# Turning a pair's outputs at the end of the odd block's list, in an AdaLN attention and expert kernel

## The reference

```
logits = h @ gate_w.T; each token goes to its 2 best of 8 experts
per (batch, expert), at most 256 tokens:
  q = (xe @ q_w.T) through two small maps, multiplied;  k likewise, with the expert's k_w;  v = xe @ v_w[e].T
  linear attention over chunks, 8 heads of 16:
    o = (q k^T * causal) v + q S;   S = S + k^T v
out[token] = sum of its two experts' rows, weighted; normalised per head; @ o_w.T
x = x + ga * out
```

## Time and profile before

| what | value |
|---|---|
| median of 3 runs (lowest, highest) | 1153.3 us (1145.38, 1154.67) |
| the profiled execution's own time | 1154.31 us |
| its span, first to last instruction | 1152.6 us |
| mean granted clock of TensorE | 0.969 |
| busy: PE, DVE, ACT, POOL | 1030.0, 903.6, 665.7, 512.3 us |

### The profile page before, as it was taken

The page is one execution under the profiler, slowest core; times in us unless marked ns, Lnnn a source line. Parts: engine busy times, 40 slices in busy tenths (PEclk is TensorE's granted clock), DMA queues, the critical chain, the costliest instruction groups (busy, mean ns, idle before and its releaser), DMA issues.

```text
span 1152.6 us, 23833 instructions
## 1 busy us (share of the span) xinstructions
PE 1030.0 (89%) x7766; PEld 721.8 (63%) x7766; DVE 903.6 (78%) x2107; ACT 665.7 (58%) x1651; POOL 512.3 (44%) x477
## 2 busy tenths in 40 slices
PE   6776888899998789999998989989998999899997
PEld 4554565566665556666665657657776677677774
DVE  5885677899985667887798877898889887877764
ACT  2543455556655566767675755646675665555563
POOL 2074154503334542132212237858886554466551
PEclk9997899999998999999999999989999999999997
DMA  9997133323333332222222233232533052214320
GB/s 301 354 399 106 56 123 108 124 76 102 107 104 101 97 94 74 69 77 74 64 72 63 56 108 111 74 101 70 139 103 101 12 158 83 80 54 115 104 71 18
DMA packets 87047, 124.00 MB, mean 108 GB/s; under 512 B 11280, under 2 KB 70160, under 8 KB 82832
## 3 DMA queue, kind: packets, MB, share of 16 engines
q1 hardware_dynamic: 76688, 97.30, 28.1%
q0 software_dynamic: 10240, 25.18, 7.6%
HBM read 71.32 MB, written 51.13 MB: 106 GB/s over the span
## 4 chain that ended last, share of the span: by engine, by line
PE 50%; DVE 27%; ACT 9%; issue 8%; another core or an unknown queue 5%; DMA 0%; DVEq 0%; POOL 0%; SPq 0%; ACTq 0%; POOLq 0%
PE bank L1433 6%; PE wide L1457 6%; PE bank L1719 5%; PE bank L1517 5%; PE bank L1709 5%; PE wide L1709 5%; DVE epp L1795 4%; PE bank L1501 3%; DVE kvw L1802 3%; DVE att L1559 2%; PE bank L1509 2%; PE bank L1420 2%; PE bank L1447 1%; ACT epp L1770 1%
## 5 line engine op out<-in xcount | busy, mean ns | idle before, releaser
L1672 POOL TENSOR_TENSOR kvw<-kvw,hq 128x512 f32<-128x512 f32 x128 | 171.3, 1338 | 150.7 <-ACT kvw L1762 150.4
L261 POOL DMA_INDIRECT routed_rows<-hq,idxs x128 | 131.2, 1025 | 232.5 <-DVE att L1559 98.7
L921 POOL DMA_INDIRECT gst<-attended_rows,idxs x128 | 135.2, 1057 | 203.4 <-DVE att L1559 100.2
L1559 DVE SCALAR_TENSOR_TENSOR att<-reach,endrel,wide 128x1024 f32<-128x1024 f32 x152 | 194.4, 1279 | 22.3 <-PE wide L1457 12.6
L1795 DVE TENSOR_TENSOR epp<-kvw,epp 128x512 fp32r<-128x512 f32 x160 | 142.9, 893 | 77.7 <-ACT epp L1770 75.6
L1719 PE MATMUL bank<-epp,w2p 128*128 128x512 f32 x480 | 162.7, 448 | 8.3 <-DVE epp L1795 8.1
L1770 ACT ACTIVATE epp<-kvw 128x512 fp32r<-128x512 f32 x160 | 100.8, 630 | 94.6 <-DVE kvw L1802 89.9
L1709 PE MATMUL bank<-hp,w1p 128*128 128x512 f32 x480 | 140.3, 401 | 0.0
L1709 PE MATMUL wide<-hp,w3p 128*128 128x512 f32 x480 | 138.5, 397 | 0.0
L1433 PE MATMUL bank<-kvw,turned 128*128 x304 | 131.1, 513 | 5.7 <-ACT turned L1321 2.7
L1762 ACT ACTIVATE kvw<-bank 128x512 f32<-128x512 f32 x160 | 94.7, 592 | 57.0 <-PE wide L1709 55.9
(11 more groups left out here) (265 smaller groups left out, 1876.6 us busy)
## 6 DMA issues: line engine op xcount, KB each, us to landing
hq<-weight_rows SPq DMA_DIRECT2D x16, 2048.0 KB
rows<-routed_rows SPq DMA_DIRECT2D x76, 256.0 KB
routed_rows<-zero SPq DMA_DIRECT2D x2, 7168.0 KB
attended_rows<-ob SPq DMA_DIRECT2D x76, 128.0 KB
routed_rows<-zero SPq DMA_DIRECT2D x1, 5120.0 KB, 19.2
out<-fin SPq DMA_DIRECT2D x16, 256.0 KB, 2.4
routed_rows<-hq,idxs POOLq DMA_INDIRECT x128
gst<-attended_rows,idxs POOLq DMA_INDIRECT x128
```

The source lines that it names most:

```text
L261: pool.indirect_dma_start(hs[s], bass.IndirectOffsetOnAxis(idxs[:, t, k:k + 1], 0), hq[:, t, :], None, bounds_check=BLOCKS[s] * P - 1, oob ...
L921: pool.indirect_dma_start(gst[:, u, k, :], None, orow[s], bass.IndirectOffsetOnAxis(idxs[:, t, k % TOPA:k % TOPA + 1], 0), bounds_check=BL ...
L1559: dve.scalar_tensor_tensor(out=att[:, n % 2, :, :], in0=reach[:, :, :].rearrange("p a c -> p (a c)").unsqueeze(1) .to_broadcast([P, 4, 2 * ...
L1672: pool.tensor_tensor(g, g, rows_of(1 - b % 2, n, n + 1), ALU.mult).then_inc(s_eu, 1)
```

## The change

`turn_outputs(h)` moves from between `keys_values` and `turn_k` to the very end of TensorE's list of an odd n, behind `carried(n+1)`. `output_rows(h)` moves from behind `split_heads` to the end of ScalarE's list, behind the post copies and the post work. ScalarE's copy of the turned k gets a semaphore of its own, `s_kk`, one count a pair. TensorE's `turn` now waits for that in place of `s_kx`, which comes after the two head copies. `turn_outputs(h)` waits until the copy of pair h + 2's turned k is done (count h + 3), where it waited for the copy `turned` of pair h + 3.

```diff
+        s_kk = sem("turned_k_copied")
...
-                act.activation(k_turned(g), bank[0][:, 0:2 * P].rearrange("p (a c) -> p a c", c=P), ACT.Copy)
+                act.activation(k_turned(g), bank[0][:, 0:2 * P].rearrange("p (a c) -> p a c", c=P),
+                               ACT.Copy).then_inc(s_kk, 1)
...
 # attention_scalar, the loop
-                if odd and here(h):
-                    output_rows(h)
                 exponent(n)
                 linear(n)
                 post_copies(act, n)
                 post_act(act, n)
+                if odd and here(h):
+                    output_rows(h)
...
 # turn(g)
-                    pe.wait_ge(s_kx, g - 1)
+                    pe.wait_ge(s_kk, g - 1)
...
 # turn_outputs(g)
                 pe.wait_ge(s_oc, g + 1)
-                pe.wait_ge(s_te, min(g + 4, PAIRS))
+                pe.wait_ge(s_kk, min(g + 3, PAIRS))
...
 # attention_tensor, the loop
-                if odd and here(h):
-                    turn_outputs(h)
                 if odd and here(h + 2):
                     turn_k(h + 2)
...
                 post_pe(pe, n)
                 if is_block(n + 1):
                     carried(n + 1)
+                if odd and here(h):
+                    turn_outputs(h)
```

## The result

The changed kernel takes 1170.0 us, the median of four runs (1158.19 to 1172.16), against 1152.2 for the one before beside it (1145.38 to 1154.67). The ratio is 1.0147, with a 95% interval of 1.0099 to 1.0195: it is slower, by 11 to 22 us. The forecast was 1161, its range 1144 to 1176: the time lies in the range, 9 us above the forecast.

A forecast was written before the change was run, and what follows sets the result against it. TensorE, busy 89%, was taken as the bound, sharing early attention with VectorE. Terms 11.8, 4.2, 1.2, -1.3 and -9.9 made +6.0 on 1154.3, 1160.3; about 1 for other pairs and the median 1 lower left 1161, range 1144 to 1176.

The forecast's parts named there:

- the hand-off: turn_outputs waits for ScalarE's k copy with scores queued behind: 0.47 late in 25 chain passages before 400 us, +11.8.
- (b): After 400 us, 7 chain passages without post work: oTs is on time, loss 0.6 each, +4.2.
- (c): Turns with the transposes of line 994, 7 passages: scores 0.17 later each, +1.2.
- (d): Turns with the Silu copy, 5 passages: turn_k 0.44 earlier, 0.25 reaching the copy and head splits, -1.3.
- (e): Output product at line 1014 comes 1.3 us earlier, so VectorE's addition at line 1059 stops waiting: -9.9, least sure.
- Rival (1): Slower: the additions' 9.9 us don't come back, plus 3 for output_rows, 1173 us; chance 0.27.
- the late rows: output_rows behind ScalarE's post work, needed by turn in the even list: 0, with +3 as the upper end.
- The rival of a hidden delay: Faster: TensorE waited for VectorE ahead of scores anyway, so idle time at line 1447 is saved; 1139 us, chance 0.12.
- The rule that I cited: Two of TensorE, VectorE, ScalarE cannot use one PSUM bank in the same partition in one cycle; wait can't be dropped.

The follow-up runs named there:

- The outer experiments: On the changed kernel: k copy put first on ScalarE, turn_outputs at the end, 1164.0 us; or turn_outputs waiting for the two head copies too, 1231.9 us.
- TensorE's half: Kernel before with only TensorE's list changed, with the signal and the waits, output_rows left behind split_heads: 1175.4 us, ratio 1.0154.

## Why the prediction was right or wrong

**The sign, the place and, nearly, the size of the hand-off were right.** The sum had +11.8 before 400 us; it is +12.0 at block 76, at 405 us before, of which some 2 to 3 us are the clock, so nearer 9 to 10 for the hand-off. It had 0.47 a pair; the turn at 329 us has 0.50 from the product to `scores`, and the early median is 0.43 more. Where the loop starts was wrong: I had it run from `oTs`'s start to `scores`, 1.24 to become 1.71, and that turn has 2.24 (331.72 - 329.48), as `oTs` comes early there and the chain does not pass it. The chain did not stay at 25 passages there, it now has 33, but they were paid less than in full. `turn_k` follows at 0.65 as forecast, the k copy starts 0.15 behind v's (0.2 assumed), and only the signal is 0.14 to 0.15 where I had 0.05. The outer experiments, removing the wait and lengthening it, both bear out that this step carries most of the loss.

**The late plain turns and the ones of line 994, (b) and (c), were right together**: +4.2 and +1.2. The post work repeats every ten lists. In such a round the intervals between masks say the following (medians over seven rounds, in us; interval 1 is the one behind the mask of block 80, 90 and so on, and has the output product, 3 the Silu copy):

| interval in the round | 1 | 3 | 4 | 5 | 7 | 8 | 9 |
|---|---|---|---|---|---|---|---|
| before | 6.44 | 3.94 | 4.71 | 3.21 | 2.68 | 3.53 | 2.80 |
| after | 6.30 | 3.91 | 4.56 | 3.20 | 3.20 | 3.03 | 3.60 |

Intervals 7 to 9 grow by 0.80 a round on the mean, 5.6 us in seven rounds, against 5.4. Number 9 is the one with line 994 of the earlier trace rows. Its own shift is small, as I had it: in that of block 109 the product stands at 538.91 and `scores` at 541.06, 2.15 apart, against 1.93 before (523.84 to 525.77), 0.22 where the sum had 0.17. The rest of what shows between its masks seems carried over from 7, as 8 looks quick.

**The Silu turns, (d), give less than half** of the -1.3: interval 3 is 0.03 shorter in the median and not shorter on the mean. The chain of the earlier trace rows goes on from the Silu copy over VectorE to the next mask, in interval 4, and that one is 0.16 shorter in the median, 0.5 us over seven rounds.

**The step that failed is (e), the output product, -9.9.** Additions still wait 7.8 us in seven turns (6.4 of it up to 692 us), so 2 us came back. All intervals but 7 to 9 together give back 1.4 us in the seven rounds, where (d) and (e) had 11.2. I had taken an unnamed releaser for TensorE's late product because that was the only signal waited for. The product did come 1.4 us earlier behind the key and value product, and the wait stayed; without the gathers it is gone. The sum without the 7.8 that stayed is 1154.3 + 6.0 + 7.8 = 1168.1, as measured. That agreement is partly luck: the clock added some 2 to 3 us up to block 76, and 2.4 were given back outside the blocks; no step of mine held either. And the range held only because it was wide: the sum had 6 us, the kernel lost 14 in the trace and 18 in the medians.

**Rival (1) named the right reason**, the signal late for another reason than the product, and gave 1173, nearer to 1170 than the forecast. By its own condition, less than 3 us of the additions' waits gone, it is the one that came true. Its 3 us for the late rows can't be seen beside TensorE's half. The rival of a hidden delay falls, since TensorE met VectorE's mask in 6 turns instead of 24.

**A misreading**: the prediction gives line 1447 2% of the chain, 23 us. The earlier trace rows says 1%; its 49 pieces add up to 16.9 us. No term used it.

**Bank 0.** The rule that I cited from the Trainium skill (Advanced Engine Details and Errata, Bank Collisions) could not be tried, as every kernel here waits the sharing out. The other one, from the Trainium skill (Perfetto Trace Analysis, Tensor Engine Instruction), a weight load ahead of matmuls in flight, would have made the loss 5 us smaller. In the turn at 329 us the load of line 1449 starts at 331.35 and its matmul at 331.38, both behind the wait, so the 0.14 was not to be had. Where no wait stands between, loads do start early: in the timeline of the early k copy that of line 1455 starts at 293.22, while the matmuls of `carried` run from 293.11 to 293.49.

**What stays open.** The kernel with the early k copy and `turn_outputs` at the end is slower than the kernel before by 0.5%, and by 4.0 us than the same kernel with `turn_outputs` at its old place. That the transposes at the end stand directly between `carried` and `scores`, with nothing left in the list to make up for them, is my reading; the wait for `oTs` that moved to `carried`, the early k copy itself and the clock are rivals, and no run isolates one. Dropping the wait for the k copy was not tried, since the two would then meet in bank 0. Nor was a third buffer for the gathered rows, which has no room in SBUF. None of the versions with all its work left in beats the kernel before.

## What to carry to other kernels

When a step is moved to the end of an engine's list, cost its new wait as a loop: which copy of the other engine's list it needs, how many stand ahead of that one, and what is queued behind the step; here three copies further down ScalarE's list lengthened the way from the product to `scores` by 0.43 us in the early pairs, which outweighed every idle gap that it closed. Then ask the same of whoever waits for the step. A wait whose releaser the profile can't name should not be booked as a gain until an experiment has made it go away: take out the suspected neighbour once, and look whether the idle time goes with it. And before a few microseconds of a trace are given to a cause, look where the granted clock was low in each.

## What the runs showed of the hardware

That indirect DMAs go with late starts on other engines was unexpected. With gathers of GpSimd running, 1.0 us each and 0.30 apart, instructions of ScalarE and VectorE that wait for TensorE start late: `oTs` with 1.80 of idle time at 547.93, the addition 3.0 us after the product's end. Leaving out 128 gathers took 41 us off the kernel, up to some 10 of them perhaps the clock's (0.974 in that run, 0.965 in the mean of the kernel before beside it), and the late starts from 340 us on with them; six stayed before 240 us, where indirect DMAs of line 261 run in close succession. GpSimd has 0% of the chain in the profile, so that view did not point there. Whether it is the write of the descriptors, the semaphores or the transfers that stands in the way, no run here shows.

TensorE's granted clock was at 1.2 GHz for 13.7 us of one execution and for 3.4 us of another in a stretch with the same instructions on every engine, and the first took 5.0 us longer there.
